# Recommender step on one core: the last tile gets buffers of its own, the first pair gathers one more field

## What is computed

```python
e = jnp.stack([tbl_0[ids[:, 0]], ..., tbl_31[ids[:, 31]]], axis=1)   # 2048 x 32 x 256
dots = jnp.einsum('bnd,bmd->bnm', e, e)                              # all pairs of fields
z = dots[:, iu, ju]                                                  # i < j: 496 values a sample
h = jnp.concatenate([z, dense_ctx], axis=1)                          # 512 values a sample
h = jnp.maximum(h @ W_top1 + b_top1, 0.0)                            # 512 -> 512
h = jnp.maximum(h @ W_top2 + b_top2, 0.0)                            # 512 -> 256
y = h @ W_top3                                                       # 256 -> 1
```

## Time and profile before

| | us |
|---|---|
| median of 3 runs | 598.65 |
| profiled execution, its own time | 599.15 |
| its span, first to last instruction | 597.6 |
| POOL busy, 432 gathers | 417.9 |
| PE busy | 514.4 |
| DVE busy | 362.2 |
| ACT busy | 266.9 |
| granted TensorE clock, mean | 0.957 of full |

### The profile page before, as it was taken

The page is one execution under the profiler, slowest core; times in us unless marked ns, Lnnn a source line. Parts: engine busy times, 40 slices in busy tenths (PEclk is TensorE's granted clock), DMA queues, the critical chain, the costliest instruction groups (busy, mean ns, idle before and its releaser), DMA issues.

```text
span 597.6 us, 16305 instructions
## 1 busy us (share of the span) xinstructions
PE 514.4 (86%) x7136; PEld 485.9 (81%) x7136; DVE 362.2 (61%) x755; ACT 266.9 (45%) x392; POOL 417.9 (70%) x438
## 2 busy tenths in 40 slices
PE   0453899999999899989999899989999799997676
PEld 0453899998989798978989798978989699986665
DVE  1444876757775766754775766754775576743332
ACT  0460545625553364533553464633553354634331
POOL 6777777777777777777777777777777777776000
PEclk9795999999999999997999999998999899998797
DMA  6997443444443443343444433343344444333000
GB/s 168 251 275 178 110 122 106 117 122 116 115 116 113 126 115 116 111 128 108 116 116 117 124 117 116 104 126 115 112 117 114 124 117 116 107 106 108 1 2 1
DMA packets 33769, 70.03 MB, mean 117 GB/s; under 512 B 13091, under 2 KB 18739, under 8 KB 33075
## 3 DMA queue, kind: packets, MB, share of 16 engines
q0 software_dynamic: 20736, 56.65, 33.4%
q1 hardware_dynamic: 12964, 12.35, 8.1%
HBM read 68.96 MB, written 0.01 MB: 115 GB/s over the span
## 4 chain that ended last, share of the span: by engine, by line
POOL 45%; PE 27%; issue 15%; DMA 7%; DVE 3%; ACT 1%; SPq 1%; POOLq 0%; DVEq 0%
POOL rows L264 45%; PE gram_ps L299 8%; PE sel_ps L359 8%; PE tr_ps L278 5%; PE gram_ps L321 4%; DMA rows<-in_tbl,ids_sb 3%; DMA sel_ids<-in_ids_by_field 3%; DVE onehot L525 2%; PE gram_ps L331 1%; ACT dots L465 1%; SPq L227 1%; PE gram_ps L310 1%; DVE emb_t L447 1%; DVE dots_t L532 0%; DVE dots L465 0%
## 5 line engine op out<-in xcount | busy, mean ns | idle before, releaser
L264 POOL DMA_INDIRECT rows<-in_tbl,ids_sb x432 | 417.2, 966 | 132.8 <-issue 128.0
L359 PE MATMUL sel_ps<-onehot,sel_high 125*128 125x256 f32 x640 | 164.0, 295 | 18.3 <-DVE onehot L525 16.1
L447 ACT COPY emb_t<-tr_ps 128x512 f32<-128x512 f32 (+1 forms) x112 | 123.7, 1108 | 93.5 <-PE tr_ps L278 92.7
L278 PE MATMUL tr_ps<-ident,rows 128*128 128x128 f32 x864 | 118.3, 281 | 46.8 <-DMA rows<-in_tbl,ids_sb 44.5
L359 PE MATMUL sel_ps<-onehot,sel_low 125*128 125x256 f32 x640 | 157.9, 285 | 0.0
L447 DVE COPY emb_t<-tr_ps 128x512 f32<-128x512 f32 (+1 forms) x112 | 119.7, 1084 | 45.5 <-PE tr_ps L278 44.7
L359 PEld LDWEIGHTS sel_ps<-onehot,sel_high 125*128 125x128 f32 x640 | 124.0, 194 | 24.0 <-issue 21.7
L278 PEld LDWEIGHTS tr_ps<-ident,rows 128*128 128x128 f32 x864 | 98.4, 144 | 53.4 <-DMA rows<-in_tbl,ids_sb 32.1
L299 PEld LDWEIGHTS gram_ps<-emb_t 128*64 128x64 f32 x4096 | 128.9, 143 | 9.9 <-issue 5.9
L299 PE MATMUL gram_ps<-emb_t 128*64 128x62 f32 x4096 | 134.3, 228 | 2.4 <-DVE hid_t L536 1.7
L525 DVE TENSOR_SCALAR onehot<-sel_ids,row_numbers 125x256 fp32r<-125x256 int32 x320 | 100.3, 381 | 57.5 <-PE sel_ps L359 35.5
(11 more groups left out here) (22 smaller groups left out, 109.3 us busy)
## 6 DMA issues: line engine op xcount, KB each, us to landing
rows<-in_tbl,ids_sb POOLq DMA_INDIRECT x432
sel_ids<-in_ids_by_field SPq DMA_DIRECT2D x40, 128.0 KB
sel_raw<-in_tbl SPq DMA_DIRECT2D x5, 896.0 KB
w_sb<-in_W_top SPq DMA_DIRECT2D x1, 1024.0 KB, 16.4
sel_raw<-in_tbl SPq DMA_DIRECT2D x5, 104.0 KB
w_sb<-in_W_top SPq DMA_DIRECT2D x1, 512.0 KB, 19.4
out_y<-hid_t SPq DMA_DIRECT2D x16, 0.5 KB
ids_sb<-in_ids SPq DMA_DIRECT2D x1, 240.0 KB, 3.0
```

The source lines that it names most:

```text
L264: pool.indirect_dma_start(out=rows[:, slot, :], out_offset=None, in_=tables[f], in_offset=bass.IndirectOffsetOnAxis(ap=ids_sb[:, t, f:f + ...
L278: last = nc.tensor.transpose(tr_ps[h][g % 2][:, j, :], rows[:, slot, h * P:(h + 1) * P], ident[:])
L359: last = nc.tensor.matmul(sel_ps[j % 2][:, h, :], table[:, i, c, h * P:(h + 1) * P], onehot[:, c, :], start=(c == 0 and table is sel_high) ...
L447: copy(emb_t[t % PAIR][:, h, :, at[0]:at[-1] + 1].rearrange("p (g s) f -> p f s g", s=QUAD), tr_ps[h][g % 2][:, 0:len(at), :].rearrange("p ...
```

## The change

1. The last tile's `dots`, `dots_t` and `hid2_t` are no longer the common ones: they lie over slots 0 to 10 of the row ring, which nothing uses once the last quad is transposed. Its four fills go to four banks (two of `sel_ps`, two of `tr_ps[0]`), its turned features and layers to `tr_ps[1]`. Its fills wait for no copy and no y.
2. `last_periods` takes the place of periods 15 and 16: the fills and layer 1 of tile 14 with the last six quads, then the four fills of tile 15, then layers 2 and 3 of tile 14, then the rest of tile 15. In `last_dots_copy` DVE and ACT each copy two of the four blocks of every fill.
3. PE is no longer four quads ahead: the start section has 7 quads, and period t holds tile t's own quads. Period 1 has 7 of them, the odd periods after it 6, the even ones 8 (the eighth is the first quad of the next tile).
4. In tiles 0 and 1 the first selected field is gathered (28 rows a tile), so that pair 0 has four jobs instead of five, after quads 1, 2, 4 and 5. Its table is loaded last.
5. The ids of all four jobs of pair 0 are loaded ahead of the tables, in a place over `dots_t`. The tables are then loaded in one go, with no wait between them, in pieces of 2 KB (two table rows) instead of 8 KB.

```diff
-AHEAD = 4
+ROWS_AT_ONCE = 2
+GATHERED_FIRST = 1
+SELECT_AFTER = (1, 2, 4, 5)
...
+    def n_gathered(t):
+        return n_rows + (GATHERED_FIRST if t < PAIR else 0)
...
-    turns_at_start = quads + AHEAD
-    turns_odd, turns_even = 6, 8
+    turns_odd, turns_even = quads - 1, quads + 1
...
+        g = t * quads + at + (t % PAIR if t > 1 else 0)
...
+        def gram_out(t, fill):
+            bank = gram_ps[fill % 2][:]
+            if t == last_tile:
+                bank = (sel_ps[fill][:] if fill < 2 else tr_ps[0][fill - 2][:]).rearrange("p a s -> p (a s)")
...
             def load_table(n):
-                table = tables[SELECTED[n]].rearrange("(p c) w -> p (c w)", c=SELECT_CHUNKS)
+                table = tables[SELECTED[n]].rearrange("(c p r) w -> p c (r w)", p=select_rows, r=ROWS_AT_ONCE)
...
-            for job in jobs(0)[:2]:
+            for job in jobs(0):
                 load_sel_ids(*job)
-            load_table(0)
-            for n in range(1, n_sel):
-                sp.wait_ge(rows_loaded[(n - 1) % quad_sems], rows_landed(n - 1) * DMA)
+            for n in range(GATHERED_FIRST, n_sel):
+                load_table(n)
+            for n in range(GATHERED_FIRST):
                 load_table(n)
...
# PE, last_periods, t = 15
+                gram(t - 1, 0)
+                turning(0)
+                gram(t - 1, 1)
+                turning(1)
+                gram(t - 1, 2)
+                gram(t - 1, 3)
+                turning(2)
+                turn(t - 1)
+                turning(3)
+                layer1(t - 1)
+                turning(4)
+                turning(5)
+                for fill in range(fills):
+                    gram(t, fill)
+                layer2(t - 1)
+                layer3(t - 1)
+                turn(t)
+                layer1(t)
+                layer2(t)
+                layer3(t)
...
# DVE, start section and the end of last_periods
+            for g in range(quads):
                 emb_copy(dve, 0, copy, g)
+                if g in SELECT_AFTER:
+                    split_table(SELECT_AFTER.index(g))
+                    job = next(next_jobs)
                     for half in range(2):
                         build_onehot(job, half)
...
+                for fill in range(fills):
+                    last_dots_copy(dve, 0, copy, fill)
+                turn_dots(t)
+                layer2_copy(dve, 0, bias_relu, t - 1)
+                y_copy(t - 1)
+                turn_copy(dve, 0, copy, t)
```

More of the change, by code:

```diff
@@ L74, in build, with places @@
     quads = -(-n_rows // QUAD)
-    def places(k):
-        return range(k * QUAD, min((k + 1) * QUAD, n_rows))
+    def n_gathered(t):
+        return n_rows + (GATHERED_FIRST if t < PAIR else 0)
+    rows_before = [sum(n_gathered(i) for i in range(t)) for t in range(tiles)]
+    assert n_gathered(0) <= quads * QUAD
+    def places(t, k):
+        return range(k * QUAD, min((k + 1) * QUAD, n_gathered(t)))
     quad_sems = RING // QUAD + 1
@@ L85, in slots @@
         t, k = every_quad[g]
[L86 to L90, removed]
+        return [(rows_before[t] + place) % RING for place in places(t, k)]
+    quad_of_row = [g for g, (t, k) in enumerate(every_quad) for _ in places(t, k)]
     def rows_landed(g):
-        return sum(len(places(every_quad[i][1])) for i in range(g % quad_sems, g + 1, quad_sems))
+        return sum(len(places(*every_quad[i])) for i in range(g % quad_sems, g + 1, quad_sems))
     def jobs(t):
@@ L257, in _ @@
                     pool.wait_ge(ids_loaded[t], DMA)
[L258 to L261, removed]
+                for slot, place in zip(slots(g), places(t, k)):
+                    j = rows_before[t] + place - RING
+                    if j >= 0 and quad_of_row[j] >= freed:
+                        freed = quad_of_row[j] + 1
                         pool.wait_ge(transposed[1], freed)
@@ L287, in gram @@
                         pe.wait_ge(sel_copied[b][u], jobs_in_bank(b, t // PAIR))
-                if turn_of_bank:
+                out = gram_out(t, fill)
+                if t == last_tile:
+                    pass
+                elif turn_of_bank:
                     pe.wait_ge(dots_copied[k], t * fills_each + turn_of_bank)
@@ L330, in layer2 @@
                     for i in range(m1):
[L331 to L332 removed]
+                        last = nc.tensor.matmul(mlp_ps(t, m)[:, 0:P], w2_sb[:, i, m * P:(m + 1) * P],
+                                                hid1_of(t)[:, i, :], start=(i == 0), stop=(i == m1 - 1))
                     last.then_inc(layer2_done[m], 1)
@@ L457, in sel_copy, with dots_block @@
                  ).then_inc(sel_copied[j % 2][u], 1)
+        def dots_block(copy, t, fill, s):
+            dots = dots_of(t).rearrange("p (f g) -> p f g", g=groups)
+            own, at = slice(s * fields, (s + 1) * fields), s % TILED * firsts
+            return copy(dots[own, :, fill * bank_groups:(fill + 1) * bank_groups].rearrange("p f g -> p g f"),
+                        gram_out(t, fill)[own, :, at:at + firsts])
         def dots_copy(eng, k, copy, t, turn_of_bank):
@@ L463, in dots_copy, with last_dots_copy @@
             for s in range(QUAD):
-                own, at = slice(s * fields, (s + 1) * fields), s % TILED * firsts
-                last = copy(dots[own, :, fill * bank_groups:(fill + 1) * bank_groups].rearrange("p f g -> p g f"),
-                            gram_out[k][own, :, at:at + firsts])
+                last = dots_block(copy, t, fill, s)
             last.then_inc(dots_copied[k], 1)
+        def last_dots_copy(eng, who, copy, fill):
+            eng.wait_ge(gram_done[fill % 2], last_tile * fills_each + fill // 2 + 1)
+            for s in range(who * QUAD // 2, (who + 1) * QUAD // 2):
+                last = dots_block(copy, last_tile, fill, s)
+            last.then_inc(dots_copied[who], 1)
         def pack_copy(who, copy, t):
+            packed = packed_of(t)
             if who == 0:
```

213 lines of the change are left out of this document (147 added, 66 removed).

## The result

The changed kernel takes 585.31 us (583.17 to 585.63, 4 runs) against 599.58 us (598.0 to 602.31) for the kernel before in the same comparison: ratio 0.975, 95% interval 0.9705 to 0.9795. The forecast was 584.9 us, range 580.5 to 591.5. The profiled execution is the quickest of the four, 583.17 us with a span of 581.1; the other three have spans near 583.3.

What follows compares the result with a forecast made beforehand. The number of POOL's gathers and what comes after the last one were taken to set the time; 2.5 - 15.7 + 0.4 - 1.15 + 1.05 - 1.4 = -14.3 took 599.15 to 584.9 us, range 580.5 to 591.5.

Steps and rivals of the forecast that it cites:

- POOL's queue sets the end: Whole kernel: POOL's gathers run without a stop, 1.25 us each; two more gathers cost +2.5 us.
- Splits hold gathers: Start, POOL beside DVE: five table splits each have one long gather, 7.9 us before and after, so 0.
- The start: Start of PE's work: first fill at some 57 us against 74.75, only gives back the lead of four quads; 0.
- The size of the pieces: Table loads at the start: smaller pieces show no loss in DMA rate; no term in the sum.
- Rival A: First fill: PE becomes the bound from a first fill at 74 us on; slower by 1% from 94 us; 4%.
- Just in time: Odd tiles' last quad, directly ahead of its fills: +1.2 us a pair, PE's 64.8 against 67.5, hidden; 0.
- Rival B: PE in every period: waits for rows cost clock, 5 us a pair, 69.8 us a pair, time 601; 5%.
- rival D: Tail: tile 14's layer 1 is late, tile 15's fills start 5 us later than thought, 589.9; 10%.
- From the last row to tile 15's fills: Tail: the stretch from landing of the last rows to tile 15's fills falls from 18.1 to 2.4 us; -15.7.
- Layer 3 in the way: Tail: layer 3 of tile 14 waits for DVE's layer2_copy and stands ahead of tile 15's turn; +1.05 us.
- Layer 1: Tail, layer 1 of tile 15: PE idles less before it, so 4.4 us instead of 5.81; -1.4 us.
- rival C: Tail: waits for rows leave PE cold, fills at half clock (+6.9) and layer 1 at 6.6 (+2.2), 594.0; 6%.

Runs made afterwards that it cites:

- one selection earlier: Changed kernel, but each table of the start is cast and split one job earlier: 583.8 us, ratio 0.9699.
- Pieces of a quarter: Changed kernel, but each of the five table splits on DVE is four instructions of 512 columns instead of one of 2048: 586.21 us, ratio 0.9761.
- best kernel: Changed kernel with tables cast and split one job earlier, splits in four instructions, layer 3 of tile 14 behind layer 1 of tile 15: 576.7 us, ratio 0.9585.
- both edits: Changed kernel with tables cast and split one job earlier and each table split in four instructions: 577.81 us, ratio 0.9619.
- two selections twice: Changed kernel, but PE does the matmuls of the first two selections of the start twice: 592.58 us, ratio 0.9868.

## Why the prediction was right, and where it was not

**POOL's queue sets the end: right.** In every row of the table the last gather comes from the first one's start (2.8 to 3.0 us), 433 steps of 1.25 us, the splits and the ring, with 0.9 to 2.3 us left over, and the end comes from the last gather and the tail. 11.7 us at the start (one selection earlier) moved the end by 1.5. The last gather was put at 553, two steps after 550.44; it came at 553.93, and 1.1 of that is the ring.

**Splits hold gathers: right, 0 taken, +0.1 measured.** Five long gathers again, 8.0 us over the plain pace against 7.9. Pieces of a quarter took 6.6 of these away, with the same bytes loaded in the start. So the instruction on DVE holds the gather, not the traffic. The Trainium skill, SBUF — State Buffer, Who interferes with whom, has both the rule that fits (two SBUF inputs against a GpSimd read) and the probe that does not; the trace bears out the rule.

**The start: wrong.** The step "the first fill at some 57 us" took 53.0 for the start of pair 1's first one-hot, from the landing of its ids, and counted nothing else. That one-hot started at 71.44. The ids were no obstacle in the changed kernel; the series of ACT copy, cast, split and selection was, 12.0 to 12.9 us for each of four jobs, and the first fill is 18 us later than forecast. The ids too were put too early: where the series is out of the way they come at 59.64. "It gives back the lead" did not hold either: the first fill starts as late as before. That its "0" came out as 1.1 us is luck: 74.9 us is just early enough, and two runs with first fills of 82.6 and 83.3 us took 7 to 8 us more. So the sign "first fill before 65 us" failed, and so did that of more waits for rows (25.6 instead of over 44.5).

**The size of the pieces: put at nothing, worth 6 to 8 us.** The prediction saw no loss by smaller pieces and named no gain. With 8 KB pieces and everything else as changed the run took 593.1 us, 7.8 more than the changed kernel (6.3 by the ratios).

**Rival A: its mechanism is real, and it was priced well.** The prediction put the decisive point at a first fill of 74 us. Measured: 63.2 and 74.9 us differ by 1.5 us at the end, 74.9 and 83.3 by 7.3. The place is another one than I named, not PE's pace up to tile 14 but POOL's ring, which is full as soon as PE is late, and the time did not come back. The signs that I had named for A and B were there in part: gathers that end their wait on PE's transposes (one of them after more than 0.30 us), and a chain of waits through PE's selections up to 290 us. I had looked at one way only by which the first fill could be late; undoing the 2 KB pieces alone brings another. Its outcome, a kernel slower than before, came in no run.

**Just in time: right.** The chain has fills of two even tiles 64.3 us apart (142.47 and 206.81), PE's own pace for a pair, forecast as 64.8 against POOL's 67.5. Rival B, a pair of 69.8 us, is not there, nor is rival D: tile 14's layer 1 ends ahead of the last two quads, and the fills of tile 15 wait 1.04 us for the last copy alone.

**From the last row to tile 15's fills: right.** -15.7 taken. Landed at 556.6 (a gather's 2.67 us after 553.93), fills at 558.56: 2.0 us instead of the 2.4 assumed and of 18.1 before. Undoing the order of the quads alone costs 9 us, undoing parts 1 and 2 alone 3.2; no run undoes both.

**The fills: +0.4 taken, -0.8 measured** (558.56 to 566.24, 7.7 us against 8.5). **Dots copy: -1.15 taken, -1.1 measured** (1.17 against 2.29). **Layer 3 in the way: +1.05 taken, +0.9 measured**, from the end of the pack at 569.37 to the turn at 570.34, against 0.1 before. **Layer 1: -1.4 taken, -2.0 measured** (3.81 against 5.81); part of it is the clock's doing in this run, as the next lines show.

**Cold clock: the forecast's side in this profile, in part C's in others.** Stretches of the fills and of layer 1, first the changed kernel, then the 8 KB kernel; the columns are those of the earlier trace rows:

```profile
558.50:566.30 7.80, 7.74 (x257) 7.71 (x258) 3.58 (x7) 3.60 (x7) 0.00 (x0) 1.00 0.02 4
...
571.50:575.40 3.90, 3.81 (x32) 3.65 (x32) 0.61 (x2) 0.01 (x1) 0.00 (x0) 1.00 0.00 0
```

```profile
567.70:577.60 9.90, 9.89 (x257) 9.83 (x257) 3.50 (x6) 3.54 (x6) 0.00 (x0) 0.75 0.01 3
...
582.90:588.40 5.50, 5.42 (x32) 5.26 (x32) 0.61 (x2) 0.01 (x1) 0.00 (x0) 0.69 0.00 0
```

There the fills came out of a wait of 1.99 us for the last row at the lower of the two levels for a part, and cost 2.2 us more; layer 1 cost 1.6 more. In the kernel with earlier splits layer 1 took 5.34 us at 0.70, which is its 28.8 in the last column. That is 3.8 us of the 9 that rival C had priced. The rule in the Trainium skill, TensorE: Matmul & The Clock Gate, HAM oscillation, that such waits cost the clock, is thus seen in this tail, though not in every run: the fills of the best kernel were slow after a wait for rows of 1.61 us, those of the kernel with both edits were not after one of 1.65. What decides between the two is open, and so is why three of four runs of the changed kernel have spans over 2 us longer than the profiled one.

**The sum.** Against before's span the terms measured are +3.5 for the last gather, -16.2 from there to the fills (4.6 us instead of 20.8), -0.8, -1.1, +0.9, -2.0: together -15.7 of the 16.5 by which the span fell (-14.3 forecast). Of the remaining 0.8 us, 0.4 are the turn (0.66 instead of 1.09 us); the rest lies behind layer 2. The start's error entered with 1.1 us only, in the term of the last gather. The medians differ by 14.3 us, as forecast, but that closeness is partly chance: in the profiled executions it is 16.0. There the fills and layer 1 came out 1.8 us better than forecast and the last gather 1.0 worse.

## What to carry to other kernels

A queue that never waits sets the end by its length; what lies before it is free only until its buffer is full, so look for the first point at which the producer must wait for a slot and how many microseconds away it is, before calling the consumer's start free. Give the last tile's work the place right behind its last input; here the order of the quads was worth more (9 us) than the buffers, banks and order of the last two periods (3 us). Two edits of which one gave 1.5 us alone and the other nothing gave 7.5 us together: each alone ran into what the other removes.

## What the runs showed that I had not expected

A VectorE subtraction with both inputs in SBUF holds an indirect gather that GpSimd starts during it until 0.8 us after the instruction's end, five times out of five in the changed kernel and four out of five before (the fifth, ends 2.2 us after it): 2.18 us for the gather beside one instruction of 2048 columns, 1.45 us at most beside the same work in four of 512, at 0.2 us more of VectorE time (2.50 against 2.29).

Table pieces of 8 KB beside gathers of 1 KB rows delay the second quad by 7.6 us against pieces of 2 KB, with the same bytes and the DMA engines as full (share 1.00 and 1.01 from 10 to 30 us).

A ring that was full four times between 56 and 91 us cost POOL 9.8 us of standing in the run with two selections twice, 8.7 more than in the changed kernel. The last gather, some 470 us later, was 8.75 us late: nothing of it was made good in between.
